# Extra bf16 products of 512 columns between TensorE's narrow products, in a two-layer graph network kernel

## The reference, cut to what matters

```python
# layer 0, for each edge
gate = silu(edge_attr @ W1.T + b1) @ W2.T + b2          # 25000 x 48
gate = gate + sum(emb[type[src]] * (emb[type[dst]] @ adaptW.T))
msg  = gate * h[dst] * (cw * node_vec[dst])[:, None]
agg  = segment_sum(msg, src) / clip(segment_sum(node_vec[dst], src), 1e-8)
x    = x + layernorm(h + agg) * gamma + beta
# layer 1, for each edge
h1   = relu(h[src] @ weight1[rel] + bias1)               # through all 8 relations
msg  = (h1 @ weight2)[rel] * norm
x    = x + relu(segment_sum(msg, dst) + bias2)
```

## Time and profile before

| | |
|---|---|
| median of 3 runs | 1531.99 us (1529.84 to 1539.69) |
| span of the profiled execution | 1526.4 us |
| PE busy, mean granted clock | 1130.4 us (74%), 0.613 |
| DVE busy | 1319.3 us (86%) |
| ACT busy | 668.1 us (44%) |
| POOL busy | 1026.1 us (67%) |
| stage one, by the loops of PE and DVE | up to about 686 us |
| POOL's adds of stage one | 212.7 us to 743.0 us |
| stage two | 743 us to about 1400 us |
| last stage | about 1400 us to the end |

### The profile page before, as it was taken

The page is one execution under the profiler, slowest core; times in us unless marked ns, Lnnn a source line. Parts: engine busy times, 40 slices in busy tenths (PEclk is TensorE's granted clock), DMA queues, the critical chain, the costliest instruction groups (busy, mean ns, idle before and its releaser), DMA issues.

```text
span 1526.4 us, 20418 instructions
## 1 busy us (share of the span) xinstructions
PE 1130.4 (74%) x5198; PEld 831.4 (54%) x5198; DVE 1319.3 (86%) x3932; ACT 668.1 (44%) x1627; POOL 1026.1 (67%) x809
## 2 busy tenths in 40 slices
PE   5889899989999899881068888887878887775000
PEld 2767677777777777771035555555555555554000
DVE  6999999999989998980289999998989899888599
ACT  2444444544445444540155555555555555554000
POOL 7655667777877787566667787877777777766000
PEclk9666655655556655655575656655565556666555
DMA  7999986666666656642445666555555555554899
GB/s 225 307 324 327 328 236 157 153 146 143 142 166 149 149 139 143 155 101 11 100 120 143 166 167 156 140 138 137 136 139 127 132 131 138 138 127 81 328 400 398
DMA packets 154391, 268.73 MB, mean 176 GB/s; under 512 B 73818, under 2 KB 90411, under 8 KB 153380
## 3 DMA queue, kind: packets, MB, share of 16 engines
q1 hardware_dynamic: 78228, 223.53, 43.8%
q0 software_dynamic: 68992, 24.64, 18.5%
q10 hardware_dynamic: 7056, 19.27, 3.1%
HBM read 194.33 MB, written 112.55 MB: 201 GB/s over the span
## 4 chain that ended last, share of the span: by engine, by line
PE 34%; DVE 20%; DMA 19%; POOL 12%; issue 10%; ACT 3%; SPq 1%; POOLq 0%; DVEq 0%; ACTq 0%
PE ps_m L572 10%; POOL agg L485 8%; DMA t<-agg,src_all 6%; PE ps_m L661 6%; PE ps_qs L572 6%; DMA lows<-low 4%; PE ps_k L647 3%; DVE same L858 2%; DMA agg<-y,once 2%; DMA agg<-ysq,once 2%; DVE t L1074 2%; DVE x L1070 2%; PE ps_k L559 2%; PE ps_k L560 2%; PE ps_qs L610 1%
## 5 line engine op out<-in xcount | busy, mean ns | idle before, releaser
L521 POOL DMA_INDIRECT agg<-sums,once x196 | 312.7, 1595 | 103.5 <-issue 79.8
L443 POOL DMA_INDIRECT nodes<-in_table,dst_all x196 | 194.9, 995 | 102.2 <-issue 51.7
L512 POOL DMA_INDIRECT t<-agg,src_all x196 | 191.5, 977 | 66.1 <-issue 53.9
L572 PEld LDWEIGHTS ps_m<-msg,same 128*128 128x128 f32 x980 | 200.8, 314 | 29.0 <-issue 29.0
L572 PE MATMUL ps_m<-msg,same 128*128 128x48 f32 x980 | 208.5, 398 | 1.0 <-issue 1.0
L647 PE MATMUL ps_k<-h_t,rw_sb 56*128 56x256 f32 x588 | 122.7, 536 | 114.0 <-ACT hid L742 91.3
L572 PEld LDWEIGHTS ps_qs<-msg,same 128*128 128x128 f32 x980 | 183.6, 289 | 2.1 <-DVE msg L950 2.1
L572 PE MATMUL ps_qs<-msg,same 128*128 128x49 f32 x980 | 180.7, 363 | 2.0 <-DVE msg L950 2.0
L485 POOL DMA_INDIRECT agg<-x,once x84 | 137.4, 1635 | 43.9 <-issue 21.7
L647 PEld LDWEIGHTS ps_k<-h_t,rw_sb 56*128 56x128 f32 x588 | 62.9, 242 | 157.1 <-ACT hid L742 115.2
L559 PE MATMUL ps_k<-types_lo,low_hot 128*128 128x392 bf16 x196 | 95.7, 488 | 52.7 <-DVE low_hot L833 51.0
(11 more groups left out here) (149 smaller groups left out, 2620.2 us busy)
## 6 DMA issues: line engine op xcount, KB each, us to landing
agg<-in_both SPq DMA_DIRECT2D x14, 2758.0 KB, 15.3
t<-agg SPq DMA_DIRECT2D x49, 784.0 KB, 5.3
kept<-kept_out SPq DMA_DIRECT2D x49, 404.0 KB
kept_in<-kept SPq DMA_DIRECT2D x49, 404.0 KB, 3.5
agg<-bias_rows SPq DMA_DIRECT2D x49, 384.0 KB
out<-t ACTq DMA_DIRECT2D x49, 384.0 KB, 5.8
rows<-in_src_rows SPq DMA_DIRECT2D x49, 256.0 KB, 4.2
rows<-in_dst_rows SPq DMA_DIRECT2D x49, 256.0 KB, 3.2
```

Source lines behind the costliest of these rows:

```text
L443: pool.indirect_dma_start(nodes[s][:, t, :], None, table, bass.IndirectOffsetOnAxis(ap=dst_all[:, c:c + 1], axis=0)).then_inc(nodes_in[b % ...
L512: pool.indirect_dma_start(t2[b % T2S][:, t, :], None, wide, bass.IndirectOffsetOnAxis(ap=src_all[:, c:c + 1], axis=0)).then_inc(ends_in[b ...
L521: pool.indirect_dma_start(agg1, bass.IndirectOffsetOnAxis(ap=once1[b % LAG1][:, t:t + 1], axis=0), sums1[b % LAG1][:, t, :], None, compute ...
L572: last = mm(ps[:, t * width:(t + 1) * width], kept_same[:, at:at + P], m[:, v, :], start=(v == t), stop=(v == TILES - 1))
```

## The change

Products whose result nobody reads are put between PE's own. Each multiplies a bf16 copy of the identity, repeated four times (512 columns), by that identity. They write the second bank of `ps_k[0]` in stage one, which is unused there, and the second bank of `ps_k[1]` in stage two. That bank is in use there, so the sums of a round get one more wait, for `relu1_done`. A block of stage one gets ten: three ahead of the first lookup, one after the second, three within the sums, one after the gate, one after `h1`, one after `centred`. A round of stage two gets six: three within the sums and three after m1. DVE makes the bf16 identity once at the start.

```diff
+        ident_bf = sb("ident_bf", [P, P], BF16)
...
+        ps_idle = ps_k[0][:, 1, :]
+        ps_idle1 = ps_k[1][:, 1, :]
...
+            spin = ident_bf[:, :].unsqueeze(1).to_broadcast([P, TILES, P])
+
+            def keep_clock(ps, n):
+                for _ in range(n):
+                    mm(ps, ident_bf[:, :], spin, start=True, stop=True)
...
-            def sums_within(ps, width, kept_same, m):
+            def sums_within(ps, width, kept_same, m, ps_spin):
                 for t in range(TILES):
                     for v in range(t, TILES):
+                        if v == t and t > 0:
+                            keep_clock(ps_spin, 1)
                         at = place(v) + t * P
...
             for b in range(NBLOCK):
+                keep_clock(ps_idle, 3)
                 if b + 1 < NBLOCK:
                     lookup(b + 1, 0)
                     lookup(b + 1, 1)
+                keep_clock(ps_idle, 1)
...
                 last.then_inc(S["gate_done"], 1)
+                keep_clock(ps_idle, 1)
                 if b + 1 < NBLOCK:
                     h1(b + 1)
+                    keep_clock(ps_idle, 1)
                     centred(b + 1)
+                    keep_clock(ps_idle, 1)
...
-                    sums_within(ps_sums1, H, same[f % 2], msg1).then_inc(S["sums1_done"], 1)
+                    need(pe, S["relu1_done"], min(e + 1, NBLOCK))
+                    sums_within(ps_sums1, H, same[f % 2], msg1, ps_idle1).then_inc(S["sums1_done"], 1)
...
                     last.then_inc(S["m1_done"], 1)
+                    keep_clock(ps_idle1, 3)
...
+            V.tensor_copy(ident_bf[:, :], ident[:, :])
```

More of the change, by code:

```diff
@@ L581, in sums0 @@
                 pe.wait_ge(S["glog_done"], b + 1)
-                sums_within(ps_s, AW, same[b % 2], msg[b % 2]).then_inc(S["sums_done"], 1)
+                sums_within(ps_s, AW, same[b % 2], msg[b % 2], ps_idle).then_inc(S["sums_done"], 1)
             h1(0)
```

## The result

The changed kernel takes 1577.9 us (median of 4 runs, 1570.9 to 1583.4) and the kernel before 1530.9 us (1517.6 to 1539.7): 1.031 times as long, with a 95% interval of 1.025 to 1.037. It is slower. The profiled span is 1569.1 us, against 1526.4, and the mean granted clock 0.775, against 0.613. So the clock did rise, and the time rose with it. Two executions among the experiments, one of e4 (1616 us) and one of e11 (2453 us), lay far above the others of their kernels; the ratios leave them out, and nothing here rests on them.

What follows compares the result with a forecast made beforehand. Stage one was taken as bound by DMA, then POOL's adds; stage two by a two-round loop through POOL, landing and PE's sums. 1526.4 - 4 + 36 = 1558 us of span, with 5.6 us around it 1564; range 1505 to 1582.

Steps and rivals of the forecast that it cites:

- the 5.6 us of the sum: Whole kernel: 5.6 us around the span, added to the predicted 1558 us of span to give 1564 us.
- So stage one ends when POOL ends.: End of stage one: POOL's adds set it; the loops of PE and DVE have about 57 us of slack.
- Stage one, the other 35 blocks: 0 us.: Stage one from 212 us on: no change, since gains end in POOL's adds and losses hide up to 57 us.
- 4 us for the first 14: Stage one's first 14 blocks: a gain of 4 us at the high clock, within 0 to 6 us.
- I expect the clock to be high in most of stage one: Stage one: extra products around PE's wait for DVE's masks raise the clock from 0.61 to 0.8 or more.
- So the sums and m1 stay at the low clock in most rounds: Stage two: the clock still falls in PE's wait ahead of k2, so extra products there cost full price.
- The first rival: Stage two: the clock stays high throughout and rounds reach POOL's 12.7 us, 1507 us in all; chance 0.22.
- 3 x 0.42 = 1.3 us, all in the two-round loop: Stage two's sums: three extra products at the low clock add 1.3 us per two rounds, 0.65 us a round.
- 15.9 of POOL and landing.: Stage two's two-round loop of 26.63 us: 15.9 us is POOL and landing, 10.7 from DVE to the copy.
- PE's own loop: Stage two, rounds without a gather wait: 12.1 us becomes 12.5 to 14.3, mattering only above the gather loop's 13.95.
- Stage two, after m1: 1.3 us low or 0.65 high: Stage two, ahead of the transposes: the three products after m1 lengthen PE's work by 0.65 to 1.3 us.
- 45 x 0.8 = 36 us: Stage two's total loss: some 45 rounds each 0.8 us longer make 36 us, bounds 29 and 45.

Runs made afterwards that it cites:

- e4: Kernel before plus only the three extra products after m1 in stage two, no wait for relu1_done: 1522.8 us, 0.998 [0.993, 1.002].
- e11: Changed kernel plus six more 512-column products in stage two, in PE's wait between k1 and k2: 1579.2 us, 1.033 [1.025, 1.041].
- e8: Extra products of stage one only, plus six of 512 columns in stage two between k1 and k2, where PE waits: 1509.4 us, 0.990 [0.981, 0.999].
- e1: Changed kernel with extra products in stage one only, stage two as in the kernel before: 1504.4 us against 1522.8, 0.988 [0.979, 0.997].
- e6: Changed kernel with stage two's 784 KB chunk load (load_wide) held back until the awaited gather has landed: 1544.5 us, 1.013 [1.003, 1.023].
- e5: Kernel before plus only the wait for relu1_done ahead of stage two's sums, no extra products: 1517.2 us, 0.996 [0.992, 0.999].
- e10: Kernel before plus one extra product in stage two's sums, the wait for relu1_done and the bf16 identity copy: 1550.6 us, 1.019 [1.014, 1.024].
- e12: As e10, one extra product in stage two's sums with the wait, plus load_wide held back until the gather landed: 1558.6 us against 1533.9, 1.014 [1.010, 1.019].
- e9: Extra products in stage one only, plus load_wide of stage two held back until the awaited gather has landed: 1509.0 us, 0.992 [0.988, 0.995].
- e7: Kernel before, no extra products, with load_wide of stage two held back until the awaited gather has landed: 1513.4 us, 0.994 [0.990, 0.997].

## Why the prediction was right, and what it mis-sized

The sign and the range held, and 1564 was 14 us too low. Of the mechanism the clock came as forecast in stage one and in those rounds of stage two that set the time, and the loss is where it was put, in stage two's two-round loop through the sums. But the larger part of what a round lost came by a wait that was priced at nothing. The 14 us are -4.3 for stage one (8.3 us gained, not 4), +12.0 for stage two (48.0, not 36), +3 behind it, and +3.2 for what lies between span and median. For the last the 5.6 us of the sum weren't start and end: a run's time is 1.8 us above its own span (1570.85 and 1569.1), and the rest is how the profiled run lies to its median.

*"So stage one ends when POOL ends."* Right: the loops end 34 us sooner, and SyncE's wait grew from 59.3 to 84.9 us.

*"Stage one, the other 35 blocks: 0 us."* And 4 us for the first 14. Too small: the first add came 1.5 us sooner, not 4, and the whole gain is 8.3 us in these traces, 10 us in the means of the experiments. I had taken POOL's run between its first and last add as fixed. It got 6.8 us shorter. That 3.6 of them lie behind 641 us, where the loops are over sooner, is measured; that lighter DMA traffic is the cause is argued only, and the 3.2 us up to there have no cause shown.

*"I expect the clock to be high in most of stage one"*: 0.89 to 0.91. The page "TensorE: Matmul & The Clock Gate" of the Trainium skill, section "Why this matters for your kernels", advises to keep TensorE busy and to leave no long idle gap between bursts. The second half agrees with the long rounds here (8.08 us of wait, then 0.50 in the sums). The first half alone doesn't raise it: the earlier trace rows had 29 us without pause at 0.50. Nor did the lookups alone, behind two pairs of which the prediction saw the clock rise: groups of four stand within those 29 us too, from 438.60, 445.59 and 453.71 us on, without a rise. What changed in stage one is that ten products of 512 columns in bf16 are added to a block; which of their properties counts no run here tells.

*"So the sums and m1 stay at the low clock in most rounds"*. Right for the rounds that set the time. In the short rounds between they run at the high one, which makes the mean clock 0.73 and gives nothing back. The first rival (1507 us) needed the high clock in the loop's own rounds. And e8 shows what it would have been worth: with half the rounds at the high clock, 1509, no better than e1.

*"3 x 0.42 = 1.3 us, all in the two-round loop"*. Too large. The sums' piece grew by 5.29 - 4.43 = 0.86 us, 0.29 for each. PE's weight loads show why: those of the narrow products start with the extra one at 1032.37 us, not behind it, so some of their time is covered.

```profile
1032.37 1.61 PEld L583 LDWEIGHTS ps_m<-msg,same 128*128 128x128 f32 x6
```

From `asum` to the copy the means grew by 0.70, 0.35 a round: 0.90 in the sums, less 0.25 in m1.

*"15.9 of POOL and landing."* This is the step that failed. I took it as unchanged. Gather to `asum` grew from 3.0 to 4.8 us (from 3.37 to 5.07 in the rounds shown), as the last gather and the chunk load now leave together; e6 takes the load away and gets 28 us back. So of +1.11 us a round about 0.35 is the way from `asum` to the copy, and the larger part is landing (0.85 a round in the two rounds shown), where I had 0.65 for the sums, 0.15 for PE's own loop and nothing for landing.

*"Stage two, after m1: 1.3 us low or 0.65 high"*, which made up to 0.35 us a round. It is nothing (e4: 0.998 [0.993, 1.002]). So is the wait for `relu1_done` (e5).

*"45 x 0.8 = 36 us"*. It was 48.0 us over 49 rounds, above my upper bound of 45. With -8.3 and +3 it makes the 43 us.

The sums and PE's own loop were priced too high and the landing at nothing, so that the total came near is in part luck. What stays open is why longer sums keep the kernel out of the even rhythm. In e1 there was no slack to take up: POOL idles 0.50 us ahead of its first add at 1018.46, of which its own issue takes 0.30, so it already waits 0.2 us for the copy, and 0.27 us more in the sums (e10, e12) lengthens the loop at once. A loop 0.3 us longer for two rounds would give 13.1 us a round. That is what e12 has in its eight rounds with `load_kept` well behind the gather; the 13.7 us of its others have the slower landing. So by these parts the longer sums cost little by themselves, and most of the loss goes with loads that leave closer to the last gather. Why they do is shown by nothing here, and neither can I say why the kernel before starts in the one rhythm or the other. A run that holds back both loads would be the test, and there is none.

## What to carry to other kernels

Products that only hold TensorE's clock up belong where the engine would wait anyway or where it isn't on the path: the ten a block in stage one ended its adds some 10 us sooner, 0.6% (e1's 0.988 has the even rhythm in it too), those behind m1 gave nothing, and the three that stand between the operands' arrival and the copy cost 3%. A higher mean clock is no evidence of a faster kernel: of the kernels here the two with the highest, e11 at 0.799 and e8 at 0.798, took 1.033 and 0.990, and e1 took 0.988 at 0.727. Before pricing a delay on a loop through several engines, look where its transfers will then stand against each other, since landing time can move more than the work that was added. And a load held back to test a collision tests only that one: list every transfer that leaves near the one that is waited for. Of the kernels measured e1, the extra products in stage one alone, has the lowest ratio, 0.988 [0.979, 0.997]; e8 (0.990) and e9 (0.992) can't be told from it.

## What was unexpected of the hardware

An extra product of 512 bf16 columns held TensorE 0.42 us at the low clock (1032.37 to 1032.79 in the timeline above), as estimated, but the six narrow products behind it took 1.15 us (1032.79 to 1033.94) where six at the pace of the eight ahead (1.72 us) would take 1.29; net it cost 0.29 us, as the mean of the three. The gather that DVE waits for landed in 2.4 us with a 784 KB load leaving 1.85 us behind it (e1), and in 5.1 us with that load leaving in the same moment. With that load out of the way it still took 3.1 to 4.2 us where a 404 KB load left 0.9 us behind it or sooner (e6, e12), and 2.5 to 2.6 us where that one left 1.13 us behind it or later (e12): a load that leaves a few tenths of a microsecond later goes with 0.6 us or more less of landing. And one kernel has two rhythms, 12.9 us a round and some 13.3, with nothing in its code to choose between them. That this is a part of the spread between its runs (1510 to 1540 us in most) is argued from e5 and e7, whose profiled runs were in the even one.
